# Silu on ScalarE in place of tanh and a VectorE product, and two buffers of masked B·C products, in a Mamba2 layer with a small mixture of experts

## The reference

```
proj = xn @ in_proj_w.T
gate, xBC, dt = split(proj)                      # 8192 | 8192 + 2*1024 | 128
xBC  = silu(causal depthwise conv over 4 tokens (xBC) + conv_b)
x, B, C = split(xBC)                             # 128 heads of 64; 8 groups of B and C, 128 wide
dt   = clip(softplus(dt + dt_bias), 0.001, 100);  A = -(1..128)
Y    = ssd(x, B, C, D, dt)                       # chunks of 128 tokens: (C B^T * exp(segment sums)) @ (x*dt),
                                                 # state carried to the next chunk, + x*D
yg   = Y * silu(gate)
s    = (yg / rms of each group of 1024) * norm_w @ out_proj_w.T
out  = x0 + s * silu(experts(xn))
```

## Time and profile before

| | us |
|---|---|
| median of 3 runs | 1792.17 |
| lowest, highest | 1789.79, 1793.70 |
| profiled execution | 1795.43 |
| its span, first to last instruction | 1793.3 |
| granted TensorE clock, mean over the span | 0.979 of full |

### The profile page before, as it was taken

One profiled execution on the slowest core, in us unless ns is written; L12 is line 12 of the kernel. 1 busy time (PEld: TensorE's weight loads), 2 busy tenths in 40 slices (PEclk: granted clock), 3 DMA queues, 4 the chain that ended last, 5 costly groups with the idle time before them and its releaser, 6 DMA issues.

```text
span 1793.3 us, 31306 instructions
## 1 busy us (share of the span) xinstructions
PE 1689.9 (94%) x9236; PEld 1318.9 (74%) x9236; DVE 1470.5 (82%) x1729; ACT 1025.0 (57%) x1601; POOL 926.5 (52%) x593
## 2 busy tenths in 40 slices
PE   7699989999899998999899989999899989999997
PEld 5477867777677776777677767777677767777775
DVE  6534697888789798989799898978898888979886
ACT  4223566666466655666566656665566656666551
POOL 3432265565465554555465555555465545555552
PEclk9799999999999999999999999999999999999999
DMA  3321222212221222112212221112121222212203
GB/s 116 118 82 67 84 80 64 62 56 65 66 68 51 63 69 63 60 53 72 65 57 56 67 71 55 59 57 74 56 69 47 72 63 63 62 54 76 67 20 141
DMA packets 73458, 121.39 MB, mean 68 GB/s; under 512 B 12366, under 2 KB 17870, under 8 KB 73252
## 3 DMA queue, kind: packets, MB, share of 16 engines
q1 hardware_dynamic: 72676, 117.92, 21.9%
q10 hardware_dynamic: 576, 1.05, 0.2%
HBM read 112.64 MB, written 6.29 MB: 66 GB/s over the span
## 4 chain that ended last, share of the span: by engine, by line
PE 69%; DVE 17%; issue 9%; ACT 3%; POOL 1%; DMA 1%; DVEq 0%; ACTq 0%; SPq 0%; POOLq 0%
PE pj L455 12%; PE pj L457 12%; PE pj L456 12%; PE ob L455 6%; PE sc L622 5%; PE ob L456 5%; PE ob L457 5%; DVE conv L1222 4%; DVE decay L1250 3%; PE seg L601 3%; PE tb L611 2%; PE sc L626 2%; DVE acc L1304 2%; DVE wo_lo L1286 2%; DVE xc L1236 1%
## 5 line engine op out<-in xcount | busy, mean ns | idle before, releaser
L959 POOL TENSOR_TENSOR w_lo<-stg,w_hi 128x512 fp32r<-128x512 f32 x316 | 501.6, 1588 | 510.2 <-ACT w_hi L827 413.5
L455 PE MATMUL pj<-xT_hi,w_hi 128*128 128x512 f32 x1208 | 488.5, 404 | 31.8 <-DVE conv L1222 28.2
L457 PE MATMUL pj<-xT_hi,w_lo 128*128 128x512 f32 x1208 | 478.6, 396 | 0.0
L456 PE MATMUL pj<-xT_lo,w_hi 128*128 128x512 f32 x1208 | 478.3, 396 | 0.0
L1222 DVE SCALAR_TENSOR_TENSOR conv<-pj,par,conv 128x510 f32<-128x510 f32 (+2 forms) x480 | 357.1, 744 | 42.2 <-ACT conv L835 30.8
L989 POOL TENSOR_TENSOR xc<-xc,thg 128x512 f32<-128x512 f32 x128 | 209.5, 1636 | 227.0 <-DVE xc L1273 227.0
L455 PEld LDWEIGHTS pj<-xT_hi,w_hi 128*128 128x128 f32 x1208 | 230.9, 191 | 95.6 <-DVE conv L1222 28.7
L1250 DVE TENSOR_TENSOR decay<-decay,gm 128x1536 f32<-128x1536 f32 x128 | 285.8, 2233 | 0.0
L457 PEld LDWEIGHTS pj<-xT_hi,w_lo 128*128 128x128 f32 x1208 | 231.2, 191 | 50.6
L456 PEld LDWEIGHTS pj<-xT_lo,w_hi 128*128 128x128 f32 x1208 | 231.3, 191 | 45.9
L455 PE MATMUL ob<-wo_hi,yT_hi 128*128 128x512 f32 x540 | 224.0, 415 | 7.0 <-DVE part L1299 4.4
(11 more groups left out here) (169 smaller groups left out, 2307.0 us busy)
## 6 DMA issues: line engine op xcount, KB each, us to landing
stg<-wstream SPq DMA_DIRECT2D x387, 256.0 KB, 2.6
rowt<-cs_scr SPq DMA_DIRECT2D x384, 4.0 KB
colt<-cs_scr SPq DMA_DIRECT2D x384, 4.0 KB
acc<-hid SPq DMA_DIRECT2D x8, 256.0 KB, 4.4
decay<-gate_scr SPq DMA_DIRECT2D x8, 256.0 KB, 4.4
xc<-hid SPq DMA_DIRECT2D x8, 256.0 KB, 5.2
out<-acc SPq DMA_DIRECT2D x8, 256.0 KB, 2.0
gate_scr<-part SPq DMA_DIRECT2D x4, 256.0 KB, 2.0
```

What stands on the lines that cost most here:

```text
L455: nc.tensor.matmul(dst, hi_w, hi_x, start=first, stop=False)
L456: nc.tensor.matmul(dst, hi_w, lo_x, start=False, stop=False)
L457: return nc.tensor.matmul(dst, lo_w, hi_x, start=False, stop=last)
L959: nc.gpsimd.tensor_tensor(w_dest(n, 1), stg[:, s % RING, :], f32(w_dest(n, 0)), ALU.subtract).then_inc(S["wl"], 1)
```

## The change

`Silu` is computed by ScalarE directly, for the gate from the bank (`gate_silu` on ACT, scale 1 and not 0.5) and for x from `conv` (`x_silu` on ACT). The two DVE products go, and with them the buffers' halving: the conv's parameters are copied unhalved, and the epsilon is EPS. The gate block's bank is now freed by ACT. ACT's table of functions has to be changed between the exponentials and Silu, and the built program holds an `ACT_TABLE_LOAD` before each such change: 260 are executed, where the kernel before executes 3. `gm` has a buffer for each half. `mask_products` moves on DVE from step 6, after `block_weights`, to step 5, after the taps. On PE `bc_products` moves in step 5 from the end to the place behind the x block, and the `exponents` of step 5 (last pair of the half) moves behind the output products and waits for both masks. On ACT the step-5 `decays` comes after the x block's Silu. On DVE the taps of a second x block come before `y_lo`.

```
-        gm = sb("gm", [P, 2, 3 * P])
+        gm = sb("gm", [P, 2, 2, 3 * P])
...
-            def bc_products(g, half, n):
+            def bc_products(g, half):
                 pe.wait_ge(S["silu"], at(g, half, NX, 2))
-                pe.wait_ge(S["exp"], at(g, half, NJ, n))
+                pe.wait_ge(S["exp"], at(g, half, NJ, -1))
...
             def exponents(g, half, n):
+                if n == NJ - 1 and not is_last(g, half):
+                    pe.wait_ge(S["gm"], at(g, half, 2, 4))
...
+                if s == 5 and not is_last(g, half):
+                    bc_products(*following(g, half))
                 if has_pair(g, half, s + 1):
                     x_turn(*pair(g, half, s + 1))
                 if has_pair(g, half, s):
                     scan(g, half, s)
-                if has_pair(g, half, s + 2):
+                if s != 5 and has_pair(g, half, s + 2):
                     exponents(*pair(g, half, s + 2))
                 if len(mine) > 1:
                     channel_block(g, half, mine[1])
                 if with_out:
                     out_of_step(g, half, s)
-                if s == 5 and not is_last(g, half):
-                    bc_products(*following(g, half), 0)
+                if s == 5 and has_pair(g, half, s + 2):
+                    exponents(*pair(g, half, s + 2))
...
-            def x_tanh(g, half, m):
+            def x_silu(g, half, m):
                 act.wait_ge(S["conv"], at(g, half, 3 * NX, 3 * (m + 1)))
-                act.wait_ge(S["silu"], at(g, half, NX, m - 1))
-                nc.scalar.activation(thx[:, m % 2, :], conv[:, m % 2, :], ACT.Tanh).then_inc(S["tanh"], 1)
+                if m < 2:
+                    dst = bc[:, m, :]
+                    act.wait_ge(S["bcp"], at(g, half, 1, 0))
+                else:
+                    dst = xc[:, m - 2, :]
+                    act.wait_ge(S["sq"], at(g, half, NJ, m - 1 - NJ))
+                    act.wait_ge(S["ylo"], at(g, half, NJ, m - 1 - NJ))
+                nc.scalar.activation(dst, conv[:, m % 2, :], ACT.Silu).then_inc(S["silu"], 1)
...
-                nc.scalar.activation(thg[:, j % 2, :], bank(g, half, ("g", j))[:, :], ACT.Tanh, scale=0.5
-                                     ).then_inc(S["tg"], 1)
+                nc.scalar.activation(thg[:, j % 2, :], bank(g, half, ("g", j))[:, :], ACT.Silu).then_inc(S["sg"], 1)
...
-                if has_pair(g, half, s + 2):
+                if s != 5 and has_pair(g, half, s + 2):
                     decays(*pair(g, half, s + 2))
                 if mine:
-                    x_tanh(*of_half(g, half, mine[0][1]), mine[0][1])
+                    x_silu(*of_half(g, half, mine[0][1]), mine[0][1])
+                if s == 5 and has_pair(g, half, s + 2):
+                    decays(*pair(g, half, s + 2))
...
             def mask_products(g, half):
                 dve.wait_ge(S["bcp"], at(g, half, 1, 1))
-                dve.wait_ge(S["w"], at(g, half, NJ, 0))
+                dve.wait_ge(S["w"], at(g, half, NJ, -NJ))
...
-                if has_pair(g, half, s):
-                    gate_silu(g, half, s)
...
-                if s == 6 and not is_last(g, half):
-                    mask_products(*following(g, half))
                 if mine:
                     taps(g, half, mine[0])
+                if s == 5 and not is_last(g, half):
+                    mask_products(*following(g, half))
...
+                for m in mine[1:]:
+                    taps(g, half, m)
                 if s >= 1 and has_pair(g, half, s - 1):
                     y_lo(g, half, s - 1)
...
-                if mine:
-                    x_silu(*of_half(g, half, mine[0]), mine[0])
...
-                for m in mine[1:]:
-                    taps(g, half, m)
-                    x_silu(*of_half(g, half, m), m)
```

More of the change, by code:

```diff
@@ L227, in build @@
             rt_hi rt_lo selr fp fw fth fau fh fhi flo fo fot fg
-            wh wl oh ol pr cps tap conv tanh silu bcp gm segs drop exp w xt xdt y u tg sg yg yhi sq sa ylo
+            wh wl oh ol pr cps tap conv silu bcp gm segs drop exp w xt xdt y u sg yg yhi sq sa ylo
             msp ms rs o pa pb acc fin xre gre outs""".split()
@@ L719, in _ @@
         def _(act):
-            for name in "tap tanh exp tg yhi sq pa".split():
+            for name in "tap silu exp sg yhi sq pa".split():
                 nc.scalar.sem_inc(S[name], 1)
@@ L853, in decays, with gate_silu @@
                 nc.scalar.activation(d[:, 0:3:2], d[:, 0:3:2], ACT.Exp, scale=-1.0).then_inc(S["exp"], 1)
[L855 removed]
+            def gate_silu(g, half, j):
                 act.wait_ge(S["pr"], index(g, half, ("g", j)) + 1)
                 act.wait_ge(S["yg"], at(g, half, NJ, j - 1))
[L858 to L859 removed]
+                nc.scalar.activation(thg[:, j % 2, :], bank(g, half, ("g", j))[:, :], ACT.Silu).then_inc(S["sg"], 1)
             def y_hi(g, half, j):
@@ L892, in step @@
                         i = 1
-                    gate_tanh(g, half, s)
+                    gate_silu(g, half, s)
                 if s >= 1 and has_pair(g, half, s - 1):
@@ L917, in step @@
                 for b in mine[1:]:
-                    x_tanh(*of_half(g, half, b[1]), b[1])
+                    x_silu(*of_half(g, half, b[1]), b[1])
             for s in range(4, NJ):
@@ L1032, in _ @@
         def _(dve):
-            for name in "conv silu gm w xdt u sg ylo ms pb acc".split():
+            for name in "conv gm w xdt u ylo ms pb acc".split():
                 nc.vector.sem_inc(S[name], 1)
@@ L1249, in block_weights @@
                 d = decay[:, n % NDEC].rearrange("p (b h) c -> p b h c", b=2)
-                nc.vector.tensor_tensor(d, d, gm[:, :, :].unsqueeze(2).to_broadcast([P, 2, 2, 3 * P]), ALU.mult
+                nc.vector.tensor_tensor(d, d, gm[:, half].unsqueeze(2).to_broadcast([P, 2, 2, 3 * P]), ALU.mult
                                         ).then_inc(S["w"], 1)
@@ L1261, in x_times_dt @@
                                         ).then_inc(S["xdt"], 1)
-            def gate_silu(g, half, j):
-                dve.wait_ge(S["tg"], at(g, half, NJ, j + 1))
-                nc.vector.scalar_tensor_tensor(out=thg[:, j % 2, :], in0=thg[:, j % 2, :], scalar=1.0,
-                                               in1=bank(g, half, ("g", j))[:, :], op0=ALU.add, op1=ALU.mult
-                                               ).then_inc(S["sg"], 1)
             def add_scan(g, half, j):
```

23 lines of the change are left out of this document (5 added, 18 removed).

## The result

The changed kernel takes 1798.22 us (median of seven runs, 1797.03 to 1800.54), the kernel before in the same comparison 1792.17. The ratio is 1.0038, interval 1.0026 to 1.0049: 0.4% slower, where 0.7% faster was forecast. The profiled execution took 1798.05 us with a span of 1795.9 and a mean granted clock of 0.983.

What follows compares the result with a forecast made beforehand. PE, busy 94%, was taken as the bound. First halves -40.4, second halves +18.9, mean square -2.7, group 0's first half +3.1, the rest +3, clock +6: total -12.1, giving 1780 us; range 1752 to 1812.

Steps and rivals of the forecast that it cites:

- The bound and where the time lies: PE sets the pace, even steps stay at 10.73 us; steps 4 to 7 of seven first halves lose 73 us.
- The price of a load: On ACT a table load takes 1.28 us and costs 1.41 in the sequence; Relu to Silu becomes 5.3.
- rival 2: On ACT a load costs 1.28 us more, for emptying the engine; even steps lengthen, about 1980 us; chance 0.07.
- The second halves: Steps 4 to 7 of seven second halves go from 39.05 to 41.75 us, +18.9, with waits of 0.8 and 2.0.
- the walk: Steps 4 to 7 timed piece by piece from step 4's transposes: first halves end at 43.7 us, second at 41.75.
- The first halves: Steps 4 to 7 of seven first halves go from 49.5 to 43.7 us, -40.4, with a mask wait of 1.4.
- The clock's term: TensorE's clock falling behind fourteen PE waits of 2.0 to 2.7 us: from 0 to 34 us, taken at +6.
- the mean square: PE's idle 0.39 us waiting for the mean square, behind the gate's product on DVE, goes seven times: -2.7.
- the first steps: First half of group 0, without output block: ACT needs 10.0 us a step, where three steps took 26.95: +3.1.
- Rival 4: ACT falls 1.3 us further behind in each of fourteen chains through engine handovers, +18: 1798 us; chance 0.15.
- Rival 1: Every PE wait over 2 us lowers the clock, fourteen at 2.4 us, +28 instead of +6: 1808 us; chance 0.13.
- Rival 3: Waits in steps 5 and 6 close; first halves come near 40 us, second stay at 39: 1730 us; chance 0.10.

Runs made afterwards that it cites:

- e2: The changed kernel with ACT's loop turn moved into the second half, between steps 1 and 2: 1797.4 us, 1.0027 of the kernel before.
- e5: The changed kernel with ACT's tap of the second x block in steps 4 and 6 ahead of the first block's load and Silu: 1735.9 us.
- e6: The changed kernel with the second x block's tap ahead of the first block's Silu, and ACT's loop turn moved into the second half: 1732.3 us.
- e12: The changed kernel with the second x block's tap ahead of the first block's load and Silu in step 4 only: 1769.4 us.
- e1: The changed kernel with Tanh in both places of Silu, so no added table loads (output not the layer's): 1713.3 us, 0.956 of before.

## Why the prediction was wrong

**The bound and where the time lies: right.** Even steps stayed at 10.75, and the two large terms, -24 and +24 us, lie in steps 4 to 7.

**The price of a load: right.** 1.28 and some 0.1 beside it, 5.35 from Relu to Silu against 5.3, ACT busy for 1362 against 1355. By the Trainium skill, page "ScalarE: Activation LUTs", section "What ACT_TABLE_LOAD costs", a drain of about 1380 ns comes on top of each load; with 257 loads between work no row shows it, and rival 2, which had its like, falls.

**The second halves: nearly right.** 42.3 against 41.75, with waits of 0.67 and 1.76 (forecast 0.8 and 2.0). The segment sums start 0.4 later than in the walk, and the last block takes 0.1 more. One of seven (43.7) lost 1.4 to the clock.

**The first halves: the step that failed** is "ACT meanwhile turns its loop (2.21), and its tap of this block, at 16.5, is in time". The turn's duration was read in a kernel without loads, and taken over; it measured 4.76. The tap came at 19.0, and the mask wait was 2.44. DVE, on which the step had put the masks' time (21.7), was idle. The segment sums were 1.5 later than in the walk, and the block behind the last wait, which the walk had at 41.0, started at 41.65 (group 7, without the turn) to 42.8, in the mean 1.45 later. From there it took 2.86 to the end of the stretch and not 2.75, and in three of seven 4.4, for the clock: 0.7 in the mean. 43.7 + 1.45 + 0.1 + 0.7 is 45.95, and 46.0 was measured.

The turn is 0.9 of the 1.45, by e2, in which it is hidden. The rest remains in e2: there DVE's `wo_lo` and `acc` take 1.8 with POOL beside them, the masks are done at 22.5, and the block starts at 41.7. The walk's times for DVE (1.7 each) thus hold with an early tap, and not with the late one, where they were 0.74.

**The clock's term: right in its sum, by luck.** +6 was forecast and 6.0 measured, but its parts were others. The prediction read from the earlier trace rows that the clock fell in three stretches before, at 1.2 us each. It fell in all seven. Group 3, which has 0.97 in the earlier trace rows, shows it too, behind the mask wait:

```profile
877.02 0.63 PE L456 MATMUL pj<-xT_lo,w_hi 128*128 128x512 f32 x1
877.45 0.63 PE L457 MATMUL pj<-xT_hi,w_lo 128*128 128x512 f32 x1
```

In three stretches eleven to thirteen products stood 0.43 apart, in the other four six to eight, so 1.2 was the difference between a long fall and a short one, and a short one was taken as none. A short one costs 1.4 to 1.55 where no later wait takes it up. After, it came in eight of the fourteen stretches; in four first halves a later wait took it up, and four paid.

**The sum.** The forecast for the profiled execution was -12.1, measured in the span +2.6, so 14.7 were missed: some 11.3 in the first halves without the clock and 4.2 in the second; the mean square, the first steps and the end make -0.8. Even with the turn hidden the kernel takes 1797, as e2 shows: the blocks come 0.9 earlier, and the clock takes some 11 us (six first halves at 1.6, a second half at 1.4) and not 6. Two terms were thus too small, the turn on the path to the masks and the price of a short fall of the clock, and mending the first alone would not have given the time.

**Rival 4** (the saving is paid back, 1798) gave the time, but not by its cause: from the first Relu of step 6 to the second, ACT's chain took 9.7 (10.0 in the walk), so small handovers added nothing there. **Rival 1** did not come true at its price: the clock cost 6 and not 34. **Rival 3** (1730) did not happen by itself, but e5 shows that the chain it doubted can be cut. The argument against it, "the two loads and the tap stand in one row on one engine", was true, and it was an order that somebody had chosen.

## What to carry to other kernels

Where a chain ends a stretch, look in each engine's order for operations in it whose output nobody on the bounding engine waits for: here that was worth 62 us in the Silu form (on ACT) and 54 in the tanh form (on ACT and DVE), while the best kernel with 288 DVE products replaced by ScalarE work (1732.3) and the best without (1731.8) take the same time. A stretch in which several engines are nearly late answers a saving on one of them with the next; test the order before the work. And read no duration of a loop's turn from a kernel whose engine had another program in the loop.

## What the runs showed of the hardware

ACT stood idle at its loop's turn for 2.0 to 3.1 us in kernels with none to 20 loads in an iteration, and for 3.9 to 5.1 in six with 32. From the branch to the next record of the queue it was 2.4 to 3.5 us in all of them; the long turns had a second stop of 2.0 to 3.0 right behind. With the loop beginning elsewhere (e2, e6) there was one stop, and it was hidden behind operations that were still running.

The granted clock did not answer to the length of a wait alone: after, the products stood 0.43 apart behind mask waits of 2.38 and 2.44 in some groups and not behind those of 2.42 in two others, behind one wait of 1.76 of second halves and not behind six like it (1.73 to 1.76), and in e12 not behind the wait of 2.37 in the row above. A fall costs 1.4 to 1.6 us at the end of a stretch, and nothing where a later wait takes up the time.

DVE's `acc` never took over 0.75 us where POOL ran nothing beside it (10 of 64 after, 12 in e1, 4 in e2, 5 before), and 1.77 or 1.78 in the median where POOL did; the weights took 1.76 at most without POOL, and up to 2.87 with it. `wo_lo`, which took 1.83 in e2 beside POOL, took 0.74 in the same step after. Relieving or delaying POOL thus changes what DVE's work costs.
